# Hardware loops against straight code in a fused two-layer network with a mixture of experts

## The reference

```python
h = edge_filter(x)                                   # (8, 256, 256), from images (8, 3, 256, 256)
h = concatenate([h, text_embedding(x_txt)], axis=1)  # (8, 384, 256): 8 images of 384 rows
h = h + attn0(layernorm(h))      # 16 heads of 16, RoPE, causal softmax, Wo, then an MLP with gelu (256-1024-256)
h = h + ffn0(layernorm(h))       # ternary weights, relu, 256-1024-256
h = h + attn1(layernorm(h))      # 16 heads of 64, 4 key heads, ALiBi slopes, softmax with 1 + sum
h = h + moe(layernorm(h))        # 8 experts, top 2, 960 rows each: silu(x Wg) * (x Wu), then Wd, scattered back
```

## Time and profile before

| | |
|---|---|
| median of 3 runs | 1967.54 us (1960.39 to 1968.27) |
| profiled execution | 1963.76 us |
| its span, first to last instruction | 1962.0 us |
| TensorE busy | 1771.4 us (90%) |
| VectorE busy | 1236.2 us (63%) |
| ScalarE busy | 963.8 us (49%) |
| GpSimd busy | 543.5 us (28%) |
| mean granted TensorE clock | 0.947 |

### The profile page before, as it was taken

The page is one execution under the profiler, slowest core; times in us unless marked ns, Lnnn a source line. Parts: engine busy times, 40 slices in busy tenths (PEclk is TensorE's granted clock), DMA queues, the critical chain, the costliest instruction groups (busy, mean ns, idle before and its releaser), DMA issues.

```text
span 1962.0 us, 35687 instructions
## 1 busy us (share of the span) xinstructions
PE 1771.4 (90%) x10970; PEld 1409.3 (72%) x10970; DVE 1236.2 (63%) x4035; ACT 963.8 (49%) x2657; POOL 543.5 (28%) x763
## 2 busy tenths in 40 slices
PE   5687999999999999899999999981499999999997
PEld 3455677676768677677777777761399998999896
DVE  6577677686777675756766776647745454545442
ACT  1355647474666666655566656540133334333431
POOL 2241423324232410111111111110424244434431
PEclk8698999999999999999999999995689999999998
DMA  6111010101001010103000010011213221221210
GB/s 204 38 36 63 1 61 0 59 1 60 32 11 56 2 33 2 33 1 91 18 15 32 32 32 24 1 43 65 84 39 111 94 76 46 79 76 64 61 39 21
DMA packets 74179, 90.05 MB, mean 46 GB/s; under 512 B 16524, under 2 KB 64311, under 8 KB 74073
## 3 DMA queue, kind: packets, MB, share of 16 engines
q1 hardware_dynamic: 61464, 67.88, 10.6%
q0 software_dynamic: 9472, 16.77, 3.0%
q10 hardware_dynamic: 3136, 4.21, 0.6%
HBM read 71.00 MB, written 25.00 MB: 49 GB/s over the span
## 4 chain that ended last, share of the span: by engine, by line
PE 74%; issue 10%; DVE 7%; POOL 2%; DMA 2%; ACT 1%; DVEq 1%; POOLq 1%; SPq 0%; ACTq 0%
PE bank L1002 17%; PE bank L1554 17%; PE bank L1569 9%; PE bank L950 6%; PE bank L934 6%; PE bank L985 6%; PE bank L906 3%; PE bank L1161 2%; PE bank L1024 2%; PE bank L961 1%; DVE probs L2229 1%; PE bank L891 1%; PE bank L907 1%; DVE at_least L2831 1%; PE bank L1537 1%
## 5 line engine op out<-in xcount | busy, mean ns | idle before, releaser
L1677 ACT ACTIVATE probs<-probs,nmax 128x128 f32<-128x128 f32 (+2 forms) x768 | 381.1, 502 | 66.4 <-DVE nmax L2229 66.2
L950 PE MATMUL bank<-cst,probs 128*128 128x128 f32 x1536 | 235.4, 280 | 18.2 <-ACT probsT L1685 8.4
L950 PEld LDWEIGHTS bank<-cst,probs 128*128 128x128 f32 x1536 | 183.2, 143 | 67.3 <-issue 22.1
L1554 PE MATMUL bank<-xeT,gate_w 128*128 128x480 f32 x768 | 188.5, 381 | 1.4 <-issue 1.4
L1554 PE MATMUL bank<-xeT,up_w 128*128 128x480 f32 x768 | 187.2, 379 | 0.0
L2324 DVE COPY probsT<-bank 128x384 f32<-128x384 f32 x256 | 141.3, 552 | 69.6 <-PE bank L950 68.4
L1569 PE MATMUL bank<-down_w,hT 128*120 128x256 f32 x1536 | 182.9, 281 | 0.0
L1569 PEld LDWEIGHTS bank<-down_w,hT 128*120 128x120 f32 x1536 | 181.6, 182 | 0.1
L1685 ACT COPY probsT<-bank 128x384 f32<-128x384 f32 x256 | 121.7, 475 | 117.4 <-PE bank L950 108.7
L3085 POOL COPY rinv<-rowsum 128x384 f32<-128x384 f32 x80 | 40.7, 509 | 499.1 <-DVE o1T L2251 294.8
L2978 DVE TENSOR_TENSOR prod<-bank,sil 128x480 f32<-128x480 f32 x128 | 83.8, 657 | 150.0 <-PE bank L1554 149.8
(11 more groups left out here) (320 smaller groups left out, 3324.4 us busy)
## 6 DMA issues: line engine op xcount, KB each, us to landing
gate_raw<-in_L_ffn_gate_w SPq DMA_DIRECT2D x8, 1024.0 KB, 4.9
up_raw<-in_L_ffn_up_w SPq DMA_DIRECT2D x8, 1024.0 KB, 6.9
down_raw<-in_L_ffn_down_w SPq DMA_DIRECT2D x8, 1024.0 KB, 5.7
img<-in_x SPq DMA_DIRECT2D x8, 768.0 KB, 5.1
residual_rows<-x SPq DMA_DIRECT2D x8, 384.0 KB, 2.5
residual_rows<-h_in SPq DMA_DIRECT2D x8, 384.0 KB, 3.8
xr<-residual_rows SPq DMA_DIRECT2D x8, 384.0 KB, 4.6
hr<-residual_rows SPq DMA_DIRECT2D x8, 384.0 KB, 3.6
```

The lines of the kernel that those rows point to most:

```text
L950: last = tr(ps[bank][:, P * q:P * (q + 1)], probs[:, n % 4, SEG[t] + P * j:SEG[t] + P * (j + 1)], ident)
L1554: last = mm(ps[bank][:, 0:HALF], w[:, wp, c, P * m:P * (m + 1)], xeT[:, xp, c, HALF * hf:HALF * (hf + 1)], start=(c == 0 and k == 0), stop ...
L1677: last = f(p, p, ACT.Exp, bias=nmax[:, n % 4, t:t + 1], scale=-1.0, accum_out=rowsum[:, where, t:t + 1])
```

## The change

The hardware loops of TensorE, ScalarE, VectorE and of the load queue are written out as straight code, by a loop of the host program that emits the body once for each turn: the five units `MID0`, the six units `MID1` and the six experts in the middle on the three engines, and the seven turns of weight loads on `sp`. The order of the instructions and all waits stay; the values of the waits become constants, and the register arithmetic and the branches go. GpSimd isn't touched. For VectorE (TensorE and ScalarE have the same edit):

```diff
-            with dve.Fori(0, MID0) as i:
-                unit(SEC_MID0, i, (i, 1), U_MID0)
+            for i in range(MID0):
+                unit(SEC_MID0, i, (None, i + 1), U_MID0)
             unit(SEC_SIX, 0, (None, MID0 + 1), U_SIX)
             unit(SEC_SEVEN, 0, (None, MID0 + 2), U_SEVEN)
             unit(SEC_EIGHT, 0, (None, B), U_EIGHT)
-            with dve.Fori(0, MID1) as i:
-                unit(SEC_MID1, i, (i, B + 1), U_MID1)
+            for i in range(MID1):
+                unit(SEC_MID1, i, (None, i + B + 1), U_MID1)
...
-            with dve.Fori(1, E - 1) as e:
+            for e in range(1, E - 1):
                 down_lowers(e)
                 hidden(EXPERT, e, e)
```

and for the load queue:

```diff
-            with sp.Fori(0, E - 1) as e:
+            for e in range(E - 1):
                 sp.wait_ge(gate_split, e + 1)
                 load_gate_up(e + 1)
```

More of the change, by code:

```diff
@@ L1450, in _ @@
             pe.wait_ge(loaded, 16 * LOADS)
-            with pe.Fori(0, MID0) as i:
-                unit(SEC_MID0, i, (i, 1), U_MID0)
+            for i in range(MID0):
+                unit(SEC_MID0, i, (None, i + 1), U_MID0)
             unit(SEC_SIX, 0, (None, MID0 + 1), U_SIX)
@@ L1455, in _ @@
             unit(SEC_EIGHT, 0, (None, B), U_EIGHT)
-            with pe.Fori(0, MID1) as i:
-                unit(SEC_MID1, i, (i, B + 1), U_MID1)
+            for i in range(MID1):
+                unit(SEC_MID1, i, (None, i + B + 1), U_MID1)
             unit(SEC_LAST, 0, (None, 2 * B - 1), U_LAST)
@@ L1577, in _ @@
             down(EXPERT, 0, 0)
-            with pe.Fori(1, E - 1) as e:
+            for e in range(1, E - 1):
                 gates(EXPERT, e, e)
@@ L1928, in _ @@
             act.wait_ge(loaded, 16 * LOADS)
-            with act.Fori(0, MID0) as i:
-                unit(SEC_MID0, i, (i, 1), U_MID0)
+            for i in range(MID0):
+                unit(SEC_MID0, i, (None, i + 1), U_MID0)
             unit(SEC_SIX, 0, (None, MID0 + 1), U_SIX)
@@ L1933, in _ @@
             unit(SEC_EIGHT, 0, (None, B), U_EIGHT)
-            with act.Fori(0, MID1) as i:
-                unit(SEC_MID1, i, (i, B + 1), U_MID1)
+            for i in range(MID1):
+                unit(SEC_MID1, i, (None, i + B + 1), U_MID1)
             unit(SEC_LAST, 0, (None, 2 * B - 1), U_LAST)
@@ L1986, in _ @@
             expert(0, lambda: x_uppers(ROUTE, 0, (1,)))
-            with act.Fori(1, E - 1) as e:
+            for e in range(1, E - 1):
                 expert(e)
```

## The result

| | before | changed |
|---|---|---|
| median of 4 runs beside each other | 1964.60 us | 1942.65 us |
| lowest and highest | 1960.39, 1968.27 | 1939.88, 1946.86 |
| ratio, 95% interval | | 0.9897 (0.9878 to 0.9916) |
| profiled execution | 1963.76 us | 1946.86 us |
| mean granted TensorE clock, profiled | 0.947 | 0.944 |

The kernel became 22 us faster by the medians and 17 us by the two profiled executions; the interval of the ratio is 16.5 to 24 us. The forecast was 14.1 us and 1951 us. The sign, the place and the mechanism of the gain were right and its size too small: the median lies 0.35 us under 1943, the low end of the range.

What follows compares the result with a forecast made beforehand. TensorE was taken to bound the kernel, with time to give back only where it idles, in the first loop behind VectorE's jumps back. 11.73 us of stalls plus 2.41 us of clock made 14.1 us, forecast 1951 us, range 1943 to 1962.

Steps and rivals of the forecast that it cites:

- What bounds it, and where it idles: TensorE idles 20 us in the first loop, none in the second or from the second expert on; VectorE's jumps back cause waits.
- The stretch from line 985 to line 961: At the first loop's four jumps back, TensorE's time between these lines falls to 1.44 us each, a gain of 11.73 us.
- The clock behind the jumps: First loop: without TensorE's idle time the granted clock doesn't fall behind the first two jumps, 2.41 us more gained.
- A: Rival, first loop: the load of xr or another engine's work replaces the jump's wait; 7 us gain, 1958 us, chance 0.12.
- B: Rival, first loop: the idle time belongs to this point of the program, not the branch; no change, 1965 us, chance 0.06.
- C: Rival, second loop and experts: sequential fetches come late, 3.0 us each; +13 us, 1978 us, chance 0.07.
- The second loop: Five jumps back vanish on each engine, but TensorE had no idle time there: zero gain, a loss not excluded.
- Register arithmetic: Both loops: computing wait values in the sequencer costs nothing; zero, with 1.4 us either way over the five units.
- The sum: Whole kernel: 11.73 + 2.41 = 14.1 us gained, forecast 1951 us.
- D: Rival, routing stage and first expert: later half-clock stretches shift against the work, 3 to 6 us either way; 1945 us, chance 0.05.

Runs made afterwards that it cites:

- slot 28: The kernel before with all loops kept, VectorE's first loop set to begin at slot 28 of a block of 128 instructions; ratio 1.0003 (0.9980 to 1.0027).
- hinted: The kernel before with one instruction more at the top of VectorE's first loop, a hint that its closing branch goes back there; ratio 0.9923 (0.9908 to 0.9938).
- both loops at slot 0: The kernel before with all loops kept, VectorE's first and second loop set to begin at the start of a block; ratio 0.9920 (0.9896 to 0.9944).
- slot 12: The kernel before with all loops kept, VectorE's first loop set to begin at slot 12 of a block of 128 instructions; ratio 0.9925 (0.9896 to 0.9954).
- xr first: The changed kernel with unit SIX's three loads of second-layer weights issued behind those of xr and hr; against the kernel before, ratio 0.9904 (0.9888 to 0.9921).
- half changed: The kernel before with only the first loop written out, on TensorE, ScalarE and VectorE, all other loops kept; ratio 0.9974 (0.9962 to 0.9986).
- slot 100: The kernel before with all loops kept, only VectorE's second loop set to begin at slot 100 of its block; ratio 1.0057 (1.0036 to 1.0079).

## Why the prediction was right where it was, and where not

- **What bounds it, and where it idles**: right. TensorE in the first loop alone, and there VectorE behind its jump back.
- **The stretch from line 985 to line 961**: forecast 11.73 us. From 4.59 + 4.33 + 4.29 + 4.28 = 17.49 us it went to 1.44 + 3 x 1.43 = 5.73, so 11.76. Right.
- **The clock behind the jumps**: forecast 2.41 us for the rest of the four units. That rest was 85.64 + 85.49 + 84.27 + 84.44 = 339.84 us. The changed kernel's periods are 85.41, 85.37, 85.69 and 85.61 us, so the rest is 342.08 - 5.73 = 336.35: 3.49 us. The clock didn't fall behind any of the places (below, the stretch behind the second, where rows 6 have 0.50). Leaving it out of the four units was right for this pair of profiles, but "without the idle time no fall" says less than it seems: at slot 28 the same idle time stayed and no fall came, so these 2.41 us are not a fixed price of the jumps. The other 1.1 us are a term that the sum had at nothing: with the clock at 1.00 TensorE is busy for 84.30 us a unit on average in straight code, against 84.63 and 84.64 us in the third and fourth unit before, while its idle time beside the jump stayed the same (1.2 us a unit in both).

```profile
355.40:358.00 2.60, 2.60 (x23) 2.13 (x19) 2.44 (x12) 1.33 (x5) 0.00 (x0) 1.00 0.97 303
```

- **What is late next** (A): didn't come. TensorE waits for xr in none of the four units; the margin of 1.0 us held. It is late in SIX, as before.
- **That it isn't the jump** (B): refuted. The wait goes when the same loop is only placed otherwise (slots 0 and 12) or hinted, and comes back with slot 28; the place in the program's work is the same in all.
- **Late fetches of straight code** (C): none. No "issue" wait on VectorE in the changed kernel is over 0.5 us. (The kernel before had two small ones of 0.6 and 0.3 us in the straight units too, which "none" in the prediction passed over.) One of 0.44 us stands at line 2144 in the third unit; TensorE waits 0.52 us for `vpad` behind it instead of 0.17, and that unit is the longest (85.69 us). Whether it is a fetch isn't shown. The Trainium skill ("Runtime: NRT & Kernel Launch", section "Instruction fetch mechanics") says that crossing a block boundary in sequence is mostly hidden; with 89 packets for TensorE instead of 39 and 80 for the small engines instead of 68, the trace agrees. I had expected some 20 more for the small engines: 13 more came in the second loop's stretch, and 4 fewer in the first's.
- **The second loop**: the step was right for the whole change (0.08 us a unit against zero), and its reason was incomplete. "Its code evidently stays where it is" was taken for a property of the loop. It was one of its place, and the place hangs on the first loop. Had only the first loop been written out, the same working would have forecast 14 us, and 5 came. The Trainium skill ("Runtime: NRT & Kernel Launch", section "Instruction fetch mechanics") puts the window on the chip at 32 KiB for most engines, in two blocks of 16 KiB, 256 instructions each. By blocks of 256 the first loop lies in the same two blocks from slot 12 as from slot 28, and here one stayed and the other waited, so the measurement decides.
- **Register arithmetic**: zero forecast, up to 1.4 us as its bound. With both loops at slot 0 a unit takes 85.67 us against 85.37 to 85.69 written out, and 59.95 against 59.87: 0.08 to 0.15 us a unit on average, some 1 us in all. It shows as TensorE's busy time: 84.57 us a unit with the loops kept, 84.30 written out.
- **The sum**: 14.1 us forecast. The first loop gave 357.33 - 342.08 = 15.25 us end to end. SIX took 82.94 us instead of 84.72, 1.8 us less. The form of the code alone doesn't decide it: 84.59 and 83.07 us stand beside each other in two profiles that keep all loops (slots 0 and 12). Most of it is where the clock falls. In the kernel before it fell behind TensorE's wait for `qk`, in work that TensorE was free to do. In the changed kernel it fell some 7 us earlier in the unit's work, and the slower matmuls only filled the time for which `qk` was awaited anyway: the 8 matmuls of line 1002 take 5.40 us instead of 3.70, and the wait of 1.75 us is gone. From the scores ahead (641.67, 628.26) to the scores behind (650.56, 637.15) both take 8.89 us, and the same 4 matmuls behind them take 1.56 us instead of 2.65.

Before (timeline of TensorE, then a window), then changed:

```profile
642.40 3.70 PE L1002 MATMUL bank<-wqkv,xTa 128*128 128x512 f32 x8
649.54 0.77 PE L891 MATMUL bank<-cst,xh_b 128*128 128x128 f32 x5 [1.75 <-DVE qk L2255]
651.71 2.65 PE L1002 MATMUL bank<-xTb,w 128*128 128x384 f32 x4
...
650.60:653.90 3.30, 3.30 (x11) 2.04 (x11) 0.42 (x1) 3.28 (x9) 3.00 (x6) 0.50 0.00 0
```

```profile
628.98 5.40 PE L1002 MATMUL bank<-wqkv,xTa 128*128 128x512 f32 x8
637.90 1.56 PE L1002 MATMUL bank<-xTb,w 128*128 128x384 f32 x4
...
630.10:633.30 3.20, 3.20 (x5) 1.17 (x4) 0.68 (x4) 1.58 (x6) 2.77 (x6) 0.50 0.00 0
```

So 1.5 of the 1.8 us hang on where the clock fell, and the other 0.3 is a shorter wait for scores (2.37 us instead of 2.65). The clock fell early in four of the five profiles with the first loop written out on three engines (not in the one with xr first) and in one of the eight others (slot 12; the one with the hint is left out, its wait is longer). So it is partly luck, and whether straight code makes the early fall likelier isn't shown. The second loop gave 0.4. These make 17.4 us, inside both intervals and near the low end of the first timing's (16.5 to 24). Whether the 1 to 5 us up to the medians' 18.7 and 22.0 are luck of the runs or an effect wasn't settled.
- **More is gained by clocks in later stages** (D): the median is near its 1945, but the two profiles show no such gain. Their 16.9 us are covered by the terms above. For the rest of the medians it is neither shown nor excluded.

## What to carry to other kernels

A hardware loop on VectorE with a body of 297 or 366 instructions, more than two blocks of 128 and less than three, stalled for 2 to 3.3 us at each jump back or not at all, and which of the two depended on the slot at which it began, so on code that stood ahead of it. By the same theory a body of over 384 instructions would stall from every slot; no run here tried one. Look for "issue" waits of the same length, once a turn, behind the loop's branch, with packets of the instruction queue in each turn; then place the loop, hint it or write it out, in this order of effort. And when one loop is changed look at all loops behind it: the kernel that was half changed gained 5 us for the wrong reason, by winning 15 and losing 11 in code that nobody had touched.

## What the runs showed of the hardware that I had not expected

- What VectorE keeps for a jump back ends between slots 378 and 394, counted from the start of the block in which the body begins; three blocks of 128 instructions fit this and the packets of 8 KB: 366 instructions from slot 12 (to 378) and from slot 0 stay, from slot 28 (to 394) they don't, nor do 297 from slot 100 (to 397). A body that doesn't stay costs about 5 packets of 8 KB a turn, so it seems to be fetched anew as a whole: (23 - 3) / 4 in the first loop, (28 - 3) / 5 in the second.
- The jump waits 3.0 to 3.3 us in the first loop and 2.0 to 2.6 us in the second. TensorE lost 2.8 to 3.2 us and 1.9 to 2.4 us (once 3.5) a turn by it.
- With the hint the body was no longer fetched anew (3 packets in four turns instead of 23), and a wait of 2.79 us stood at the exit of the loop.
- About the same idle time of TensorE ahead of the same matmuls was followed by a granted clock of 0.53 and 0.50 at the first two jumps in the kernel before (3.08 and 2.82 us idle), and by 1.00 at all four with the loop at slot 28 (2.79 to 2.87 us).
- The jumps back of TensorE (bodies of 549, 374 and 443 instructions) and of ScalarE (202, 149 and 78) held nobody in any run.
